# Cross-attention and mixture of experts: pages of two 64-row units, gate and up transposed, down weights fetched by SyncE

## The reference

```python
x = x + xattn(layernorm(x), ctx)            # 16 heads of 8, 64 keys for each batch
t = layernorm(x).reshape(4096, 128)
shared = silu(t @ sg.T) * (t @ su.T) @ sd.T                  # inner width 128
scores = sigmoid(t @ gate_w.T) + gate_bias                   # 64 experts in 8 groups
mask   = groups among the 4 with the largest maximum
w, i   = top_k(scores * mask, 6);  w = w / (w.sum() + 1e-8)  # 6 experts a token
h      = silu(t @ eg[e].T) * (t @ eu[e].T)                   # inner width 64
routed = sum over the 6 of w * (h @ ed[e].T)
return x + (shared + routed)
```

## Time and profile before

| | |
|---|---|
| three runs, us | 680.75, 683.12, 690.93 |
| median, us | 683.12 |
| the profiled execution, us | 687.18 |
| its span, first to last instruction, us | 685.4 |
| mean granted clock of TensorE | 0.801 |

### The profile page before, as it was taken

The page is one execution under the profiler, slowest core; times in us unless marked ns, Lnnn a source line. Parts: engine busy times, 40 slices in busy tenths (PEclk is TensorE's granted clock), DMA queues, the critical chain, the costliest instruction groups (busy, mean ns, idle before and its releaser), DMA issues.

```text
span 685.4 us, 11587 instructions
## 1 busy us (share of the span) xinstructions
PE 487.6 (71%) x3208; PEld 380.1 (55%) x3208; DVE 394.0 (57%) x1925; ACT 322.2 (47%) x854; POOL 457.7 (67%) x493
## 2 busy tenths in 40 slices
PE   3877487778777877349688768777776888878720
PEld 2655265556555645239576646656665776767520
DVE  4238578878888796685234233345654554664552
ACT  3558366767666664242145344333433344444320
POOL 3001657777777777777167777777777777777772
PEclk9999779978998796559779788888878676786875
DMA  7822333333333343221333233345654555564522
GB/s 172 279 97 75 114 107 119 122 122 119 121 122 121 122 159 137 92 74 56 95 75 76 64 74 77 99 145 160 204 153 154 152 177 153 166 180 137 159 72 61
DMA packets 85262, 85.03 MB, mean 124 GB/s; under 512 B 21926, under 2 KB 72114, under 8 KB 85200
## 3 DMA queue, kind: packets, MB, share of 16 engines
q1 hardware_dynamic: 69744, 58.49, 28.9%
q0 software_dynamic: 14336, 25.52, 11.1%
q10 hardware_dynamic: 1120, 0.28, 0.2%
HBM read 39.49 MB, written 48.92 MB: 129 GB/s over the span
## 4 chain that ended last, share of the span: by engine, by line
PE 27%; POOL 24%; issue 22%; DMA 10%; DVE 8%; ACT 7%; SPq 1%; POOLq 1%; DVEq 0%; ACTq 0%
POOL pages L409 14%; POOL results L435 9%; PE bank_s L1015 8%; DMA results<-y_s,codes 6%; PE bank_o L1015 6%; PE bank_s L1086 3%; PE bank_q L1011 2%; PE bank_s L1091 2%; PE bank_q L1015 2%; PE bank_s L1011 2%; POOL rstd L399 1%; DMA y_s<-in_ctx 1%; DVE h_t L973 1%; ACT xn L508 1%; ACT y_s L603 1%
## 5 line engine op out<-in xcount | busy, mean ns | idle before, releaser
L435 POOL DMA_INDIRECT results<-y_s,codes x256 | 250.4, 978 | 93.8 <-issue 69.2
L409 POOL DMA_INDIRECT pages<-payload,place_i x96 | 92.9, 967 | 34.4 <-issue 26.7
L409 POOL DMA_INDIRECT pages<-pg,place_i x96 | 92.8, 967 | 33.2 <-issue 26.8
L603 ACT ACTIVATE y_s<-bank_o,scales 128x128 f32<-128x128 f32 x256 | 73.0, 368 | 80.3 <-PE bank_o L1015 80.3
L1015 PE MATMUL bank_o<-w_d,h_t 64*128 x512 | 89.0, 324 | 17.5 <-DVE h_t L973 17.5
L1015 PE MATMUL bank_s<-w_gu,pxt 128*128 x512 | 98.4, 351 | 3.6 <-ACT pxt L455 0.8
L1015 PEld LDWEIGHTS bank_o<-w_d,h_t 64*128 64x128 f32 x512 | 75.7, 224 | 31.7 <-issue 31.6
L1015 PEld LDWEIGHTS bank_s<-w_gu,pxt 128*128 128x128 f32 x512 | 84.1, 248 | 16.4 <-issue 15.8
L973 DVE COPY h_t<-bank_q 64x256 f32<-64x256 f32 x128 | 53.9, 421 | 47.9 <-PE bank_q L1011 47.0
L959 DVE TENSOR_TENSOR h_s<-bank_s,s_act 128x256 f32<-128x256 f32 x64 | 27.2, 425 | 86.2 <-ACT s_act L613 85.6
L1011 PE MATMUL bank_q<-ident,h_s 128*128 128x128 f32 x128 | 32.0, 337 | 52.4 <-DVE expert_i L935 52.3
(11 more groups left out here) (176 smaller groups left out, 938.3 us busy)
## 6 DMA issues: line engine op xcount, KB each, us to landing
pg<-pages SPq DMA_DIRECT2D x64, 262.0 KB, 3.0
pages<-empty SPq DMA_DIRECT2D x21, 786.0 KB
p_t<-results SPq DMA_DIRECT2D x8, 768.0 KB, 4.8
empty<-results SPq DMA_DIRECT2D x8, 768.0 KB
results<-y_s,codes POOLq DMA_INDIRECT x256
raw_w<-in_L_ffn_eg_w SPq DMA_DIRECT2D x16, 128.0 KB
raw_w<-in_L_ffn_eu_w SPq DMA_DIRECT2D x16, 128.0 KB
raw_w<-in_L_ffn_ed_w SPq DMA_DIRECT2D x16, 128.0 KB
```

The lines of the kernel that those rows point to most:

```text
L409: pool.indirect_dma_start(out=pages[:, :], out_offset=bass.IndirectOffsetOnAxis(ap=place_i[n % 2][t][:, k:k + 1], axis=0), in_=payload[n % ...
L435: pool.indirect_dma_start(out=results[:, :], out_offset=bass.IndirectOffsetOnAxis(ap=codes[j][:, g:g + 1], axis=0), in_=y_s[j][:, g, :], i ...
L603: scaled = act.activation(y_s[j][:, g, :], bank_o[:, g * D:(g + 1) * D], ACT.Identity, scale=scales[j][:, g:g + 1])
```

## The change

A page now holds two units of 64 rows, each of one expert. 64 + 384 = 448 units fit in 224 pages, 56 quads instead of 64. In the host's part of the program weights and context are laid out transposed beforehand, so `w_gu`, the shared weights, the gate and the context are loaded as they are used. With this go all transposes of weights and context on TensorE and their copies.

`w_d` is no longer on chip. For each quad SyncE reads the packed expert numbers of the lower and the upper units and issues eight DMAs, one a unit, of 64 rows of 128 numbers into `d_now`, one of three buffers (`load_down`). The gate and up weights of the eight units are copied from `w_gu` to `gu_now`: the lower units' by VectorE (`fetch_lower`), the upper units' by ScalarE (`fetch_upper`). TensorE has these weights stationary and the 64 columns of a unit moving, so gate and up come out transposed, and the transposes of `h` go. The two halves of `h_t` lie in different partitions with zeros elsewhere, so that one `down` matmul a page serves both of its units. The weights are applied in `combine`, as six chained multiply-adds a tile, and the results are copied to `y_s` in one piece.

On VectorE `find_rows` has one step more. In bodies 1 to 4 (`filling`) the order of work is another: VectorE finds the places before it takes the maxima, TensorE and ScalarE take x2 and the logits ahead of the scores, and GpSimd scatters both halves of batch 1 before the next power. The `codes` have eight buffers instead of four. The diff, cut to its core:

```diff
-PAGES = E + B * TOK * TOPK // P
+U = P // 2
+MOST_OPENED = TOK // U
+HALVES = P // U
+PAGES = (E + B * TOK * TOPK // U) // HALVES
 NQ = PAGES // QUAD
-CODE, EXPERT, WEIGHT = D, D + 1, D + 2
-PC = D + 3
+CODE, EXPERT = D, D + 1
...
+FILLS_AHEAD = 1 + (E // HALVES - FIRST_FILL) // FILL + 1
+FIRST_SUM = E // HALVES // QUAD + 2 * FILL // QUAD + 3
...
+UPFRONT = 5
...
             for w in range(B):
-                sp.wait_ge(wd_done, w + 1)
-                load_raw(w)
+                sp.wait_ge(xn2_ready, TPB * (w + 1))
+                load_experts(w)
                 if UPFRONT + w < FILLS:
                     prefill(UPFRONT + w)
...
+            def load_down(q):
+                sp.wait_ge(packed, q + 1)
+                if q >= 3:
+                    sp.wait_ge(y_done, q - 2)
+                for h in range(HALVES):
+                    v = nc.values_load(expert_i[q % SLOTS][h * U:h * U + 1, 0:1], engines=(mybir.EngineType.SP,), min_val=0,
+                                       max_val=E ** QUAD - 1,
+                                       skip_runtime_bounds_check_because="it packs four results of max_index over E experts")
+                    for g in range(QUAD):
+                        sp.dma_start(d_now[q % 3][h * INTER:(h + 1) * INTER, g, :],
+                                     expert_d[:, bass.ds((v // E ** g) % E, 1), :].rearrange("p e h -> p (e h)")).then_inc(down_in[q % 3], 16)
...
                 if q >= SLOTS:
                     sp.wait_ge(code_ready, q - SLOTS + 1)
+                    sp.wait_ge(pxt_done, q - SLOTS + 1)
                 sp.dma_start(pg[j][:, :, :], quad_v[q:q + 1, :, :, :].rearrange("a p g c -> (a p) g c")).then_inc(page_in[j], 16)
+                if q == SLOTS - 1:
+                    load_down(0)
+                    load_down(1)
+                elif q >= SLOTS:
+                    load_down(q - 2)
...
-                if n == 0:
+                if 0 <= n < 2:
                     scatter(n, 1)
                 if any_norm(b + 1):
                     inverse_deviations(b + 1)
-                if n > 0:
+                if on(n) and n >= 2:
...
+            def fetch_upper(q):
+                act.wait_ge(packed, q + 1)
+                v = nc.values_load(expert_i[q % SLOTS][U:U + 1, 0:1], engines=(mybir.EngineType.Activation,), min_val=0,
+                                   max_val=E ** QUAD - 1,
+                                   skip_runtime_bounds_check_because="it packs four results of max_index over E experts")
+                e = [(v // E ** g) % E for g in range(QUAD)]
+                if q >= 2:
+                    act.wait_ge(gu_done, q - 1)
                 for g in range(QUAD):
+                    copied = copy(gu_now[q % 2][:, g, 1, :], w_gu[:, bass.ds(e[g], 1), :].rearrange("p e i -> p (e i)"))
...
+                more = full
+                for m in range(2, MOST_OPENED + 1):
+                    chained(("opens", m), dve.scalar_tensor_tensor(out=opens[:, :], in0=filled_to[:, :], scalar=float(m * U),
+                                                                   in1=more[:, :], op0=ALU.is_gt, op1=ALU.add))
+                    more = opens
...
+            def places_first(b):
+                shifts(b)
+                if on(b - 3):
+                    find_rows(b - 3)
+                    for t in range(TPB):
+                        pick_rows(b - 3, t)
+                        places_to_int(b - 3, t)
+                both_maxima(b)
+                sum_inverse(b - 1)
+                divide_by_sum(b - 1)
...
+            def pack_experts(q):
+                j = q % SLOTS
+                dve.wait_ge(page_in[j], 16 * (q // SLOTS + 1))
+                if q > 0:
+                    dve.wait_ge(packed, q)
+                if q >= SLOTS:
+                    dve.wait_ge(upper_ready, q - SLOTS + 1)
+                    dve.wait_ge(down_in[(q - SLOTS) % 3], 16 * HALVES * QUAD * ((q - SLOTS) // 3 + 1))
+                dve.tensor_tensor(digits[:, :], pg[j][:, :, EXPERT].bitcast(I32), digit[:, :], ALU.mult).then_inc(digits_done, 1)
+                dve.wait_ge(digits_done, q + 1)
                 with nc.allow_low_precision(reason="whole numbers below 2 ** 24 are exact in float32"):
                     dve.tensor_reduce(expert_i[j][:, :], digits[:, :], AX.X, ALU.add).then_inc(packed, 1)
+            def fetch_lower(q):
+                dve.wait_ge(packed, q + 1)
+                v = nc.values_load(expert_i[q % SLOTS][0:1, 0:1], engines=(mybir.EngineType.DVE,), min_val=0,
+                                   max_val=E ** QUAD - 1,
+                                   skip_runtime_bounds_check_because="it packs four results of max_index over E experts")
+                e = [(v // E ** g) % E for g in range(QUAD)]
+                if q >= 2:
+                    dve.wait_ge(gu_done, q - 1)
+                for g in range(QUAD):
+                    copied = dve.tensor_copy(gu_now[q % 2][:, g, 0, :], w_gu[:, bass.ds(e[g], 1), :].rearrange("p e i -> p (e i)"))
+                copied.then_inc(lower_ready, 1)
...
                 xt = xb[:, n, :]
-                dve.tensor_tensor(xt, routed[:, t, :], xt, ALU.add).then_inc(summed, 1)
+                for k in range(TOPK):
+                    if k > 0:
+                        dve.wait_ge(added, (TOPK - 1) * n + k)
+                    part = dve.scalar_tensor_tensor(out=xt, in0=ys[b % YS_SLOTS][:, t, k, :], scalar=weight[:, n, k:k + 1], in1=xt,
+                                                    op0=ALU.mult, op1=ALU.add)
+                    part.then_inc(added if k < TOPK - 1 else summed, 1)
...
+            def quad(q):
+                if 0 < q < NQ - 2:
+                    pack_experts(q + 2)
+                if q > 0:
+                    take_codes(q)
+                dve.wait_ge(act_ready, q + 1)
+                if q >= 2:
+                    dve.wait_ge(y_done, q - 1)
+                for h in range(HALVES):
+                    dve.tensor_tensor(h_t[q % 2][h * INTER:(h + 1) * INTER, :, h, :],
+                                      gu_ps[q % 2][INTER:2 * INTER, :].rearrange("p (g h t) -> p g h t", g=QUAD, h=HALVES)[:, :, h, :],
+                                      s_act[:, :, h, :], ALU.mult).then_inc(h_ready, 1)
+                if q == 0:
+                    take_codes(0)
+                    pack_experts(1)
+                    fetch_lower(1)
+                    pack_experts(2)
+                if q + 2 < NQ:
+                    fetch_lower(q + 2)
+                combine_next(q)
...
+            def filling_body(b):
+                values(b - 1)
+                if on(b - 3):
+                    count_choosers(b - 3)
+                transpose_x(b + 2)
+                if on(b - 2):
+                    transpose_x2(b - 2)
+                    logits(b - 2)
+                transpose_back(b - 1)
+                transpose_max(b)
+                first_products(b)
+                transpose_o(b - 1)
+                shifted_scores(b)
+                out_projection(b - 1)
+                project(b + 2)
+                scores(b + 1)
...
+            def gate_up(q):
                 pe.wait_ge(pxt_ready, q + 1)
+                pe.wait_ge(lower_ready, q + 1)
+                pe.wait_ge(upper_ready, q + 1)
+                for u in range(HALVES * QUAD):
+                    g, h = divmod(u, HALVES)
+                    last = mm(gu_ps[q % 2][:, u * U:(u + 1) * U], gu_now[q % 2][:, g, h, :], pxt[q % 2][:, u * U:(u + 1) * U])
...
+            def down(q):
+                pe.wait_ge(h_ready, HALVES * (q + 1))
+                pe.wait_ge(down_in[q % 3], 16 * HALVES * QUAD * (q // 3 + 1))
+                if q >= 2:
...
+                    last = mm(y_ps[q % 2][:, g * D:(g + 1) * D], h_t[q % 2][:, g, :, :].rearrange("p h t -> p (h t)"), d_now[q % 3][:, g, :])
...
+            for q in range(NQ):
+                gate_up(q)
+                if q + 1 < NQ:
+                    page_x(q + 1)
+                if q == 0:
+                    down(0)
+                elif q > 1:
+                    down(q - 1)
```

More of the change, by code:

```diff
@@ L607, in quads @@
-            def quads(i, first, last):
-                for j in range(SLOTS):
-                    q = i * SLOTS + j
-                    act.wait_ge(gu_done, q + 1)
-                    if not (first and j == 0):
-                        act.wait_ge(h_ready, q)
-                    act.activation(s_act[:, :, :], gu_ps[j % 2].rearrange("p (g u i) -> p g u i", g=QUAD, u=2)[:, :, 0, :],
-                                   ACT.Silu).then_inc(act_ready, 1)
-                    if j + 1 < SLOTS:
-                        page_x(q + 1, j + 1)
-                    elif not last:
-                        page_x(q + 1, 0)
-                    if first and j == 0:
-                        page_result(0, 0, True)
-                    elif j > 0 and not (first and j == 1):
-                        page_result(i, j - 1, first)
-                page_result(i, SLOTS - 1, first)
```

(65 more changed lines are left out.)

378 lines of the change are left out of this document (159 added, 219 removed).

## The result

| | before | after |
|---|---|---|
| median, us | 682.8 (4 runs, 680.75 to 690.93) | 824.14 (4 runs, 821.71 to 827.07) |
| the profiled execution, us | 687.18 | 824.83 |
| its span, us | 685.4 | 822.8 |
| mean granted clock | 0.801 | 0.61 |

The ratio is 1.204, with an interval from 1.197 to 1.210: the change makes the kernel 141 us slower. The forecast was 715, slower by 5%, with a range up to 775. The direction came out right and the size did not.

A forecast was written before the change was run, and what follows sets the result against it. GpSimd bounds the kernel before; SyncE would bind at 6.6 us a quad. First page read 320.8, then packing, weight loads and page reads to 694.6, plus a 22.4 tail: 717.0 span, 715 median; range 660 to 775.

The forecast's parts named there:

- SyncE becomes the bound: Page stage: SyncE's queue needs 6.6 us a quad, over GpSimd's 5.15; chance 0.43 at about 6.6, giving 715.
- signs named beforehand: Profile after: scatters in fours, 6.6 us apart; weight DMAs 0.43, starts 0.64 apart; landing waits at down; first page read 315 to 326.
- second rival: Page stage: SyncE bounds with dearer reads, addresses or issues, 7.7 us a quad, 777 us; chance 0.16.
- third rival: Page stage: GpSimd stays the bound, SyncE under 5.15 us a quad; 636, or 633 as a median; chance 0.08.
- the fourth: Page stage: TensorE bounds at 1.2 GHz, 6.1 us a quad, about 689; SyncE or TensorE at 5.7 to 6.3 together 0.33.
- The price of a quad in SyncE's queue: Page stage: weight DMAs 5.13, two reads 0.81, page read 0.47, result reads and stores 0.2; together 6.6 us.
- high end of 0.78: Page stage: dear price per weight DMA, 0.49 to issue plus an extra address operation; eight make 6.25 us a quad.
- high end of 7.7: Page stage: SyncE's dearest quad, 7.7 us, with eight weight DMAs at 0.78 each.
- The stage ahead: Attention stage: 10 us taken from an expected gain of 5 to 15, so first page read at 320.8 instead of 330.8.
- I take back the two waits: Attention stage: GpSimd's waits of 5.0 and 2.8 us go, plus 2 to 6 us ahead of the first scatter.
- The tail: After the last weight DMAs: landing 3.0, down 1.4, copy 0.6, scatters 5.1, span end 11.8, combines 0.5; 22.4 us.
- The rule on issuing: SyncE's queue: by the skill's rule issuing would not bind; ranked second because nine or ten issues a quad add up.

The follow-up runs named there:

- e2: Changed kernel with both register reads of a quad ahead of its eight weight DMAs: 807.48 us, ratio 1.177 to the kernel before.
- e3: Changed kernel with ScalarE issuing the upper units' four weight DMAs, SyncE keeping four and one read: 662.19 us, ratio 0.966 to the kernel before.
- e1: Changed kernel with build-time weight DMA addresses, no register reads or arithmetic, wrong experts' down weights: 712.44 us, ratio 1.039 to the kernel before.
- e4: Changed kernel with bodies 1 to 4 in the order of the kernel before: 820.24 us, ratio 1.195 to the kernel before.
- e8: Changed kernel with build-time weight addresses and each expert's 64 rows contiguous in HBM, wrong down weights: 908.41 us, ratio 0.974, on a slower chip.
- e9: Changed kernel with down weights on chip, copied by VectorE and ScalarE, no weight DMAs: 895.17 us, ratio 0.960 to the kernel before, slower chip.

## Why the prediction was right and wrong

**SyncE becomes the bound: right, and shown.** Its queue has 1.7 us of waits in 464 (the trace after), of 0.27 us a quad cut from it 0.23 come out (e2), and half of the weight DMAs moved to another queue bring GpSimd's 1.29 us a scatter back (e3). Of the signs named beforehand, the scatters in fours, the starts spread by one quad of SyncE and TensorE's wait for landings at `down` (135 us in all) were there; the first page read at 315 to 326 was not, and the weight DMAs cost 0.48 with starts 0.76 apart, not 0.43 and 0.64. What came is the second rival, SyncE at a higher price, and higher than its 777. The third rival (GpSimd stays the bound) is what e3 shows once SyncE is relieved, and the fourth (TensorE) was not the bound in the changed kernel or in e1 to e4.

**The price of a quad in SyncE's queue: the step that failed.** I had 6.6 us; over the 464.2 us from the first page read to the end of the last weight DMA and 56 quads it is 8.29. Term by term, each the sum of the durations of that row divided by 56:

| term, us a quad | forecast | measured |
|---|---|---|
| issuing eight weight DMAs | 3.44 | 3.96 |
| arithmetic for eight addresses | 0.93 | 0.89 |
| a MOVE for each, not in the forecast | 0 | 0.24 |
| two register reads | 0.60 | 1.19 |
| a page read | 0.36 | 0.48 |
| result reads and stores | 0.20 | 0.22 |
| gaps between instructions | 1.08 | 1.31 |
| sum | 6.61 | 8.29 |

The reads are the largest miss, 0.59. I took TensorE's 0.30; on SyncE the first of a pair took 0.43 and the second, behind a DMA, about 0.7. The Trainium skill (DMA: Bandwidth & Descriptors, Latency and other measured facts) gives a floor of about 600 ns for `tensor_load`. The second reads, at about 0.7, agree with it; the first ones, at 0.43, and the 0.27 of e3 lie below, and the measurement decides. With 0.6 us a read the forecast would have been 748, nearer, and still 76 us short. The second miss is the issue: 0.52, from 0.43 to a mean of 0.495. The one row of 64 partitions, 0.49, stood in the earlier trace rows, and I gave it up for the one of 128. The arithmetic was right. A weight DMA with all that belongs to it, 0.76 us, stayed just inside my high end of 0.78. The reads and the page read had no high end at all; they took 0.71 us a quad more than forecast (0.59 and 0.12). With 0.76 a DMA and the rest as forecast, 8 x 0.76 + 1.48 = 7.56, within the high end of 7.7; these 0.71 carry it to 8.27. So the range, up to 775, lacked a dear price for the reads, and a start that is late instead of early.

**The stage ahead.** I had the first page read at 320.8, 10 us early, and it came at 336.1, 5.3 late. The failed step is "I take back the two waits". The first one, 4.96, is 6.99: in both orders twelve scatters and a power stand ahead of it, and with the first scatter 4.0 us earlier the places of batch 1 came only 1.9 earlier. The second, 2.84 ahead of a power, is gone, and 6.30 ahead of batch 2 has come in its place, since now all twelve scatters of batch 1 stand ahead of the next power, and VectorE's place finding for batch 2 behind it. With the old order the median is 3.9 us lower (e4), of which the trace shows 1.9 to 3.0 at batch 2. The rest of the 15 is for the most part the gain that wasn't there: with the old order and without the transposes the stage ends where it did before. Only the first scatter came earlier, by 1.3 us in e4 and by 4.0 with the new order (I had 2 to 6), and that was lost again by batch 2.

**The tail: right in sum.** 22.4 forecast; from the end of the last weight DMA (800.3) to the end of the span (822.8), 22.5.

The sum closes. Against a forecast of 717.0 for the span, the start costs 15.3, the page stage 464.2 instead of 373.8, so 90.4, and the tail 0.1: 717.0 + 105.8 = 822.8.

**GpSimd, TensorE, ScalarE and VectorE.** None of them is the bound, as forecast. TensorE, at a granted clock of 0.50, is busy for 37.24 / 50 x 8.20 = 6.1 us a quad; the forecast had 5.9 for the passes at that level.

**The rule on issuing.** The Trainium skill (DMA: Bandwidth & Descriptors, Issuing engines are not separate DMA queues) says that initiating a DMA is usually short beside the DMA itself. For one page read the trace agrees: 0.52 us to issue it, 3.2 from issue to landing. Nine to ten issues a quad in one queue were the bound all the same. Ranking that rule second was right.

## What to carry to other kernels

Before moving data from on-chip copies to many small DMAs, add up the issuing queue as if it were an engine: in this kernel a DMA at a computed address took 0.76 us of it (0.495 the issue, 0.112 the arithmetic, 0.029 a MOVE, 0.123 in gaps), so eight of them exceed a 5.15 us stage, however early they are issued. When such a queue is the bound, split it over a second engine's queue before giving the idea up: that alone turned 1.204 into 0.966 here, on one chip. And where a term of such a sum is taken from another engine's row, as the register reads were, give it a dear end of its own: they took twice the price.

## What the runs showed of the hardware that was not expected

- One register read has three prices on SyncE: 0.27 us in a queue with pauses (e3), 0.43 in a full one, about 0.7 right behind a weight DMA (0.686 the median in the changed kernel).
- Issuing a 64-row DMA took 0.484 in the median with address arithmetic between two of them and 0.596 without (e1, e8): the distance from one start to the next fell only by 0.12 in the median (0.76 to 0.64), though arithmetic, MOVE and two gaps, some 0.22 us, no longer stood between them.
- TensorE was granted 0.50 in the changed kernel from 500 to 550 us (37.2 of 50 busy) and 0.83 in e3 (39.2 busy), for the same products a quad, done in 8.2 and in 5.3 us.
- Programs with the same code up to the page stage had their first page read at 332.7 (e2), 336.0 (e3), 336.1 (after) and 339.3 (e1). A difference of a few us in the whole time is therefore no proof for an edit in another part.
- On three of four chips the kernel before took a third longer (914 to 933 us beside 686), with ScalarE pausing some 9 us at a time ahead of `p_t`, 16 times (141.8 / 16, e9). A ratio can't be carried from one chip to another: splitting the issues gave 0.966 on the first, and with the old order 0.995 and 0.993 on two others.
